# A two-layer graph network on one core: the first layer gathers from a list without its closing loop edges, closed up on the chip, and adds each node's own term from SBUF

## What is computed

```python
# first layer, then x = layernorm(x + feats @ W + b)
m = relu(feat[src]) + 1e-7
a = softmax of m over the edges of each dst, feature by feature
feats = feat + segment_sum(a * m, dst)
# second layer, then x = layernorm(x + h_out)
score = exp(clip(sum over the head of K[src] * Q[dst] / sqrt(12) * (edge_attr @ We + be), -5, 5))
h_out = segment_sum(V[src] * score, dst) / (segment_sum(score, dst) + 1e-6)
```

## Time and profile before

| quantity | value |
|---|---|
| time, median of 3 runs | 4857.5 us (4850.16 to 4858.55) |
| span of the profiled execution | 4892.4 us |
| instructions | 43885 |
| first layer, from the first gather to its last one's start | 2.90 to 2383.50 us |
| second layer's first gather | 2404.94 us |
| busy: POOL, PE, DVE, ACT | 64%, 63%, 47%, 18% of the span |

### The profile page before, as it was taken

One profiled execution on the slowest core, in us unless ns is written; L12 is line 12 of the kernel. 1 busy time (PEld: TensorE's weight loads), 2 busy tenths in 40 slices (PEclk: granted clock), 3 DMA queues, 4 the chain that ended last, 5 costly groups with the idle time before them and its releaser, 6 DMA issues.

```text
span 4892.4 us, 43885 instructions
## 1 busy us (share of the span) xinstructions
PE 3098.1 (63%) x13152; PEld 2767.9 (57%) x13152; DVE 2300.2 (47%) x5605; ACT 870.5 (18%) x1966; POOL 3143.9 (64%) x3330
## 2 busy tenths in 40 slices
PE   3445444555555455455578777878777877877777
PEld 3344434444444444444477677767677777767676
DVE  5434344334433443344445555555555555555555
ACT  1222222222222222222201111111111111111111
POOL 6666666666666666666566666666666666666665
PEclk8666666666656667656665655565666565566665
DMA  3111111121111111111244444444444444444443
GB/s 97 40 40 43 42 39 40 40 45 40 40 44 41 39 40 45 40 39 40 67 111 111 114 112 114 112 111 117 112 111 111 114 112 114 112 114 110 115 113 98
DMA packets 290371, 383.51 MB, mean 78 GB/s; under 512 B 154382, under 2 KB 196911, under 8 KB 290127
## 3 DMA queue, kind: packets, MB, share of 16 engines
q0 software_dynamic: 132864, 251.83, 21.4%
q1 hardware_dynamic: 157263, 128.81, 9.5%
HBM read 360.62 MB, written 19.72 MB: 78 GB/s over the span
## 4 chain that ended last, share of the span: by engine, by line
POOL 31%; issue 23%; PE 18%; another core or an unknown queue 15%; DVE 9%; DMA 2%; ACT 2%; DVEq 0%; SPq 0%; ACTq 0%
POOL rows L454 31%; PE banks L605 4%; PE banks L586 4%; PE banks L577 4%; PE banks L547 3%; DVE onehot L817 2%; PE banks L596 2%; DMA rows<-in_x,src_i 1%; DVE sums L942 1%; DVE ex L930 1%; DMA rows<-key_value,src_i 1%; DVE banks L850 1%; ACT onehot_t L717 1%; DVE sums L940 1%
## 5 line engine op out<-in xcount | busy, mean ns | idle before, releaser
L454 POOL DMA_INDIRECT rows<-key_value,src_i x1661 | 1571.9, 946 | 922.2 <-issue 431.8
L454 POOL DMA_INDIRECT rows<-in_x,src_i x1661 | 1570.6, 946 | 811.6 <-issue 469.1
L547 PE MATMUL banks<-ex,onehot 128*128 128x192 f32 x3322 | 1036.0, 483 | 1026.7 <-DVE ex L930 810.5
L547 PEld LDWEIGHTS banks<-ex,onehot 128*128 128x128 f32 x3322 | 865.2, 288 | 1188.8 <-DVE ex L930 933.9
L586 PE MATMUL banks<-qw,onehot_t 128*128 128x192 f32 x1664 | 609.2, 515 | 401.2 <-ACT onehot_t L717 233.1
L605 PEld LDWEIGHTS banks<-onehot,vals 128*104 128x104 f32 x3322 | 601.2, 272 | 260.2 <-issue 210.3
L605 PE MATMUL banks<-onehot,vals 128*104 128x64 f32 x3322 | 608.2, 359 | 183.8 <-issue 151.5
L586 PEld LDWEIGHTS banks<-qw,onehot_t 128*128 128x128 f32 x1664 | 440.3, 302 | 449.1 <-ACT onehot_t L717 258.4
L577 PE MATMUL banks<-we_sb,ea 97*128 97x96 f32 x3322 | 672.1, 372 | 0.0
L577 PEld LDWEIGHTS banks<-we_sb,ea 97*128 97x128 f32 x3322 | 662.2, 295 | 0.0
L930 DVE SCALAR_TENSOR_TENSOR ex<-banks,ex 128x384 f32<-128x384 f32 x416 | 229.0, 550 | 795.7 <-issue 654.5
(11 more groups left out here) (107 smaller groups left out, 1480.4 us busy)
## 6 DMA issues: line engine op xcount, KB each, us to landing
ea<-in_edge_t SPq DMA_DIRECT2D x415, 192.0 KB
rows<-in_x,src_i POOLq DMA_INDIRECT x1661
rows<-key_value,src_i POOLq DMA_INDIRECT x1661
qw<-query SPq DMA_DIRECT2D x832, 24.0 KB
key_value<-qkv SPq DMA_DIRECT2D x24, 400.0 KB
x<-in_x SPq DMA_DIRECT2D x7, 672.0 KB, 8.2
query<-qkv SPq DMA_DIRECT2D x24, 192.0 KB
out<-outs SPq DMA_DIRECT2D x24, 192.0 KB
```

Of the source, the lines that this page charges most:

```text
L454: pool.indirect_dma_start(out=to[0:n, r, u, :], out_offset=None, in_=table, in_offset=bass.IndirectOffsetOnAxis(ap=src_i[0:n, g * G + u:g ...
L547: last = nc.tensor.matmul(ps_sum0[b], onehot[:, r, u, :], ex[:, b, u, :], start=u == 0, stop=u == n - 1)
```

## The change

1. The edges from group PLAIN = 44 on (edge 22,528) are cut into 128 runs of RUN = 1485 edges, one per partition, the last one filled up with 108 spare loops. Two tables of these runs and the first node of each run are new inputs; SP loads them at the start, behind the weights (three DMAs).
2. During groups 2 to 40 of the first layer DVE works on them between its other instructions. `find_ends` packs source and (dst - first node of the run) in one integer and zeroes the closing edge of each node. `close_up` moves each kept edge down by the number of dropped ones ahead of it, in BITS = 7 steps of powers of two, four instructions each over 1485 elements. PE turns the closed-up runs over (`turn_runs`, 11 transposes), and `list_edges` makes the new source list `src_c`, lanes, group bases and a set of checks from it. A run keeps at most CAP = 1408 edges, so the rest of the first layer has NC0 = 352 groups of four full tiles in place of 372.
3. Each engine's If over the first layer ends at group 44; a second one, on the new flag `unequal`, holds the rest and the second layer. From group 44 POOL gathers by `src_c`, waiting for `s_sum` >= g - PACE + 1 as before.
4. For each chunk ACT computes the own terms (relu and exp of `x1`, `own_terms`), and DVE adds them to the ring just ahead of `messages` (`add_own`). The order of the node work is written for the new groups (`last0`, `at0`, `stage0`); the first four chunks come at groups 46, 54, 62 and 70.
5. DVE's tables of lanes and halves at the start cover 44 groups in place of 416, and the zeroing of `qw` moves to group 45. `qw`, `prod`, `vals` and `outs` become parts of one buffer, `late`, which the work of point 2 uses first.

The second layer's code is as before.

```diff
+PLAIN = 44
+E0 = PLAIN * G * P
+RUN = -(-(EDGES - E0) // P)
+PADR = RUN * P - (EDGES - E0)
+BLK = 11
+CAP = BLK * P
+NC0 = P * BLK // G
+NG0 = PLAIN + NC0
+BITS = 7
+LOW = 14
...
+            sp.dma_start(run_dst[:, :], run_dst_in).then_inc(s_runs, 16)
+            sp.dma_start(packed[:, :], run_src_in).then_inc(s_runs, 16)
+            sp.dma_start(run_first[:, :], run_first_in.to_broadcast([P, P])).then_inc(s_runs, 16)
...
-                for g in range(R0, NG):
+                for g in range(R0, PLAIN):
                     pool.wait_ge(s_sum, min(g - PACE, 2 * (g - R0)) + 1)
                     gather(g, g % R0, xr, x, s_row[g % R0])
+                pool.nop(nofuse=True)
+            with pool.If(1 - unequal(pool, POOL_ENGINE)):
+                pool.wait_ge(s_list, 1)
+                for g in range(PLAIN, NG0):
+                    pool.wait_ge(s_sum, g - PACE + 1)
+                    gather_listed(g)
...
+                    if g == 27:
+                        turn_runs()
...
+                def own_terms(c):
+                    n = tiles_of_chunk(c)
+                    if c:
+                        act.wait_ge(s_owned, c)
+                    nc.scalar.activation(own[:, 0:n, D:W0], x1[:, first_tile(c):first_tile(c) + n, :],
+                                         ACT.Relu).then_inc(s_ownr, 1)
+                    act.wait_ge(s_ownr, c + 1)
+                    nc.scalar.activation(own[:, 0:n, 0:D], own[:, 0:n, D:W0], ACT.Exp,
+                                         bias=gneg[:, :]).then_inc(s_own, 1)
...
-            V.memset(qw[:, :, :], 0.0)
+            V.memset(bound[:, :], 0.0)
...
+                    if g == 2:
+                        dve.wait_ge(s_runs, 48)
+                        link(V.tensor_tensor(step_to, run_dst[:, 1:RUN + 1], run_dst[:, 0:RUN], ALU.subtract))
...
+                def find_movers(k):
+                    link(V.tensor_scalar(bit, packed, 2 ** (LOW + k), None, ALU.bitwise_and))
+
+                def lift_movers():
+                    link(V.scalar_tensor_tensor(out=moved[:, 0:RUN], in0=bit, scalar=0.0, in1=packed,
+                                                op0=ALU.is_gt, op1=ALU.mult))
+
+                def leave_others():
+                    link(V.tensor_tensor(stays, packed, moved[:, 0:RUN], ALU.subtract))
+
+                def set_movers(k):
+                    to = packed if k < BITS - 1 else packed_f
+                    last = V.tensor_tensor(to, stays, moved[:, 2 ** k:2 ** k + RUN], ALU.add)
...
+                for g in range(PLAIN):
+                    weigh_rows(g)
...
+                    if g < 9:
+                        find_ends(g)
+                    elif g < 27:
+                        close_up(g)
                     else:
...
+                        list_edges(g)
...
+                def add_own(c, n_added):
+                    n = tiles_of_chunk(c)
+                    part = own[:, 0:n, 0:D]
+                    dve.wait_ge(s_own, c + 1)
+                    if c < RINGC:
+                        link(V.tensor_tensor(part, part, unlike[:, c * CT:c * CT + n].unsqueeze(2).to_broadcast(
+                            [P, n, D]), ALU.mult))
+                    link(V.scalar_tensor_tensor(out=own[:, 0:n, D:W0], in0=own[:, 0:n, D:W0], scalar=EPS_MSG,
+                                                in1=part, op0=ALU.add, op1=ALU.mult))
+                    dve.wait_ge(s_add, n_added)
+                    V.tensor_tensor(slots(c, n), slots(c, n), own[:, 0:n, :], ALU.add).then_inc(s_owned, 1)
+                    dve.wait_ge(s_owned, c + 1)
...
-                        if last_group(c) == at:
-                            dve.wait_ge(s_add, at + 1)
+                        if at0(c) - 1 == at:
+                            add_own(c, min(at + 1, NG0))
+                        if at0(c) == at:
+                            dve.wait_ge(s_add, min(at + 1, NG0))
                             messages(c)
```

More of the change, by code:

```diff
@@ L150, in build @@
         flag = sb("flag", [1, 1], I32)
+        ends = [0]
+        for size in (RE * 2 * D, 2 * G * D, 2 * G * W1, 2 * CT * D):
+            ends.append(ends[-1] + size)
+        qw = late[:, ends[0]:ends[1]].rearrange("p (a b) -> p a b", b=2 * D)
+        prod = late[:, ends[1]:ends[2]].rearrange("p (a b c) -> p a b c", b=G, c=D)
+        vals = late[:, ends[2]:ends[3]].rearrange("p (a b c) -> p a b c", b=G, c=W1)
+        outs = late[:, ends[3]:ends[4]].rearrange("p (a b c) -> p a b c", b=CT, c=D)
+        spread = qkv[:, :, :, :].rearrange("p a b c -> p (a b c)")
+        beside = rows[:, :, :, :].rearrange("p a b c -> p (a b c)")[:, R0 * G * D:R0 * G * D + RUN]
+        run_dst = late[:, RUN:2 * RUN + 1].bitcast(I32)
+        packed = late[:, 0:RUN].bitcast(I32)
+        packed_f = late[:, 0:RUN]
+        step_to = beside
+        bit = beside.bitcast(I32)
+        moved = spread[:, 0:RUN + 2 ** (BITS - 1)].bitcast(I32)
+        stays = late[:, RUN:2 * RUN].bitcast(I32)
+        listed = beside[:, 0:CAP].bitcast(I32)
+        dst_c = late[:, RUN:RUN + CAP].bitcast(I32)
+        lane_c = spread[:, 0:CAP].bitcast(I32)
+        span_c = spread[:, 0:CAP]
+        empty = late[:, 0:CAP]
+        done0 = spread[0:1, RUN + 64:RUN + 64 + NG0].bitcast(I32)
+        base_f = spread[0:1, RUN + 64 + NG0:RUN + 64 + NG0 + NC0]
+        ahead0 = ahead[0:1, 0:NG0]
         xr = rows[:, :, :, :].rearrange("p a b c -> p (a b c)")[:, 0:R0 * G * D].rearrange(
@@ L457, in gather_tile, with gather_listed @@
                 ).then_inc(s, 16)
+            def gather_listed(g):
+                for u in range(G):
+                    t = (g - PLAIN) * G + u
+                    pool.indirect_dma_start(
+                        out=xr[:, g % R0, u, :], out_offset=None, in_=x,
+                        in_offset=bass.IndirectOffsetOnAxis(ap=src_c[:, t:t + 1], axis=0)
+                    ).then_inc(s_row[g % R0], 16)
             def gather(g, r, to, table, s):
@@ L540, in turn_sums, with sum_rows @@
                 last.then_inc(s_z, 1)
-            with pe.If(1 - irregular(pe, PE_ENGINE)):
[L543 to L549, removed]
+            def sum_rows(g):
+                b, r = g % 2, g % RO
+                pe.wait_ge(s_p, g + 1)
+                for u in range(G):
+                    last = nc.tensor.matmul(ps_sum0[b], onehot[:, r, u, :], ex[:, b, u, :],
+                                            start=u == 0, stop=u == G - 1)
+                last.then_inc(s_sum, 1)
@@ new lines, in slot_values, with add_rows @@
+            def slot_values(g):
+                return nc.values_load_multi_w_load_instructions(
+                    halves[0:1, g:g + 2, :].rearrange("p a b -> p (a b)"),
+                    engines=[DVE_ENGINE], min_val=0, max_val=(SLOTS - 1) * W0,
+                    skip_runtime_bounds_check_because=why)[1]
+            def add_rows(g, low, high):
+                dve.wait_ge(s_sum, g + 1)
+                if g:
+                    dve.wait_ge(s_add, g)
+                else:
+                    dve.wait_ge(s_zero, 1)
+                acc = sums0[0:WIN, bass.ds(low, W0)]
+                V.tensor_tensor(acc, acc, ps_sum0[g % 2][0:WIN, :], ALU.add)
+                acc = sums0[WIN:P, bass.ds(high, W0)]
+                V.tensor_tensor(acc, acc, ps_sum0[g % 2][WIN:P, :], ALU.add).then_inc(s_add, 1)
```

347 lines of the change are left out of this document (268 added, 79 removed).

## The result

The changed kernel takes 4768.3 us (median of 4 runs, 4765.5 to 4773.5) against 4858.0 us for the kernel before: a ratio of 0.982, 95% interval 0.9806 to 0.9834, or 89.7 us less. The forecast was 4774.5 us, with a range from 4743 to 4815 us.

A forecast was written before the change was run, and what follows sets the result against it. The first layer was taken as bound by POOL's gather issue plus pauses for late PE sums. Terms -110.2 - 3.9 + 16 + 4 + 3 + 2 + 3 + 3 = -83 us gave 4774.5 us, range 4743 to 4815 us.

The forecast's parts named there:

- What the change removes: First layer: 77 fewer gathers at 1.432 us each, -110.2 us; less DVE table work at the start, -3.9 us.
- the pauses go by PE's instructions: Both layers: pauses come every 44 to 47 PE matmuls, not by time, so left-out groups take their share along.
- the prediction's alternative price of 1.248 us: First layer: price per gather if only POOL's issue were saved and not the pauses, -96 us for 77 gathers.
- The start: Before the first exponential: moving `qw` zeroing and shrinking tables from 1664 columns to 176 saves 3.9 us, at least 0.
- Closing up: DVE in the first 44 groups: 85 us of added work, of which 16 us shows, between 0 and 40.
- the catch-up: Groups 9 to 13, POOL waiting for sums: 18.5 us added against 8.4 us free on DVE, 10 us late.
- Its rule: DVE instructions of one input and a constant can hold up POOL's gathers: five instructions, +4 us, 0 to 12.
- No slack behind group 13: First layer: the 10 us late at group 13 are never made up, as the pace has no slack against POOL's issue.
- The Ifs: Group 44: four engines load a flag and branch, +2 us, 0 to 8.
- rival C: Second layer gets longer as its pauses shift to 3.8 us each: +333 us, 5107 us; chance 5%.
- the prediction's sign of being wrong: Second layer: a length that moved by more than 10 us would show the forecast wrong.
- rival B: First 44 groups: the preparation sets the pace, 85 us shows in place of 16, 4843 us; chance 15%.

The follow-up runs named there:

- the run meant for it: Three in place of four one-hot products per group from group 44 on, against the changed kernel, gathers kept: 4135.5 us, ratio 0.9862 (chip 15).
- the run without it: Changed kernel without the closing-up work, 20 whole groups of the old list skipped instead, own terms kept: 4753.6 us, ratio 0.9791 (chip 9).
- the two idle kernels: Kernel without closing up plus 37 idle 1.7 us DVE instructions: sums of two SBUF tables 4143.8 us, reductions of one table 4123.1 us (chip 15).
- the run in PSUM: Changed kernel with the closing up working on a table in four PSUM banks: 4121.1 us, ratio 0.983 (chip 0).
- another edit in the same run: Changed kernel with closing up in PSUM and POOL five groups ahead of the sums instead of three: 4771.8 us, ratio 0.9818 (chip 1).

## Why the prediction was right, by its own steps

**What the change removes.** The term that carries the result, 77 gathers at 1.43 us, came out: from group 44 to the last gather it is -108.6 us between the two profiles of one chip, against -110.2 + 3 + 2 = -105 us forecast for that stretch. That a left-out group takes its share of the pauses with it is shown by the equal price of a gather on chip 9 (1.423 us in both kernels). That the pauses go by PE's instructions wasn't shown: the run meant for it fell on a chip without them. On such a chip a gather costs 1.258 us, near the prediction's alternative price of 1.248 us, and there the change brings 56 us. The prediction knew of one kind of chip only, and that the change was measured on the same kind was luck: where there are no pauses, 56 us would have come of the forecast 83.

**The start.** The first relu begins at 34.38 us in place of 37.61, so DVE's shorter tables gave 3.2 of the 3.9 us. On chip 9 they were lost again: POOL's first gather of group 9 starts at 55.01 us against 55.68 us in the second profile of the kernel before, behind a pause of PE that ends at about the same time in both.

**Closing up.** At group 44 the forecast had -3.9 + 16 + 4 + 3 = +19 us, and +11.2 us was measured. At group 13 the kernel was late by 8.6 us already (88.63 against 80.00 us), so the catch-up was indeed the costly part. The sum of the terms was too large: the preparation costs 9 to 12 us by the run without it, for 23. And the hold-ups were misread. The prediction put 16 us on DVE's order and 4 us on five gathers held up by instructions of one input and a constant, and priced the 21 instructions of `close_up` with two inputs as if gathers didn't mind them. Its rule is right as far as it goes (the gather at 105.43), but 42 gathers take over 1.0 us in the first 44 groups and not five, 21 of them under those 21 instructions. The row that showed it was there: the gather of 1.85 us at 16.74 began under L797, an instruction with two SBUF inputs, and not only under the cast behind it. The step that failed is that reading. How much it is worth depends on the bound: on the chips without pauses 20.7 us between the two idle kernels and 15.5 us back in PSUM, on the chips with pauses 2.8 us at group 44, with another edit in the same run. So how the 9 to 12 us divide into hold-ups and DVE's order there isn't shown.

**No slack behind group 13.** The prediction held that what is late there is never made up, as POOL's issue had no slack. Where the pauses are, the sums set the rate and POOL has some room: the first 176 gathers take 190.6 us against 169.8 us in the kernel before, and those 21 us, together with DVE's order, came to 11 us at group 44. On the chips without pauses the statement fits: the run in PSUM is 13.7 us ahead of the changed kernel at group 44 and 15.5 us at the end.

**The Ifs, the own terms, the second layer.** POOL's first listed gather follows with 0.30 us of idle time as any other: 0 us for the 2 us forecast. The own terms cost 0.7 us by the run without them, for 3; without pauses they weren't left out, and the 13 us of held-up gathers behind group 44 may show there. Between the layers +2.7 us, for +3. The second layer +0.4 us, for 0; rival C is out. Only the first pair of profiles set off the prediction's sign of being wrong (22 us in the second layer), by its long execution. The carry-over from the span to the median, with 35 us between them, was right because that execution was long throughout.

**The sums.** -83 us were forecast, and -89.7 and -94.3 us were measured; the preparation, 8 to 14 us too dear, is most of the difference. Three figures of the prediction don't come out of its own terms. With the own terms at 20 us the high end is 4791.5 us, with the held-up gathers at 12 and the preparation at 40 it is 4806.5 us, and with all three 4823.5 us, but not 4815. Half of rival B's 85 us gives 4801 us and not 4808. And five iterations of `close_up` hold eight instructions, 13.6 us at 1.7 us each and not 14.4. Nothing in the result hangs on them.

**Open.** Why sums are late on two chips and not on the other two isn't settled. Nor is it shown that the chip is the reason, for each was used in one set of runs only. What is shown is the place (the wait on PE's sums), the rate (5.7 us per group) and that POOL's lead doesn't change it. In the timeline with five groups ahead the products are recorded as done at 1009.19 (1008.70 + 0.49), and POOL and DVE, which wait for their sums, go on at 1014.09 and 1014.30. Two things narrow it. The traces hold all 3168 products of the first layer on either kind of chip, but only 291 of the 396 updates of the sums' semaphore on chip 9 against all 396 on chip 0 (the changed kernel). As every time here is of an execution whose span and clock were recorded too, a part of the recording in these waits can't be excluded. And fetching of code, which the prediction named as a possible reason, is not in step with them: between 1000 and 1300 us the kernel before has 12 waits of POOL over 1 us and 10 packets of instructions (chip 9), the changed kernel on chip 0 has none and 13.

## What to carry to other kernels

Before work is put into the idle time of DVE, look at what runs beside it: here an indirect gather on GpSimd was held up by DVE instructions that took both inputs from SBUF, and by the one-input form that takes 0.94 us for 1485 columns. The same instructions with an input in PSUM left it alone. Price a term by what bounds the stage, and check the profiled execution's span against the median before subtracting two profiles, since here it was long by 35 us. A gain from fewer gathers is worth what the bound on that chip makes of it, 94 us or 56 us for one program, and so is a remedy for held-up gathers, which brought 15.5 us where POOL is the bound and nothing that shows where it isn't.

## What the runs showed of the hardware that was not expected

The kernel before runs at 4857 us on two chips and 4193 us on two others, and in the first layer of the changed one the difference shows as POOL's waits for PE's sums: a gather costs 1.42 us on the first two and 1.26 us on the others. The changed kernel's second layer takes 2452 and 2077 us. A gather that begins under a DVE instruction of 1485 columns with two SBUF inputs takes 1.1 to 2.4 us and mostly ends about 0.8 us behind it (95.40 + 1.70 and 96.46 + 1.45 above). One that begins under the one-input form of 0.94 us does the same (105.15 + 0.93 and 105.43 + 1.45). One beside a reduction of 1.7 us, or beside the same instructions with an input in PSUM, takes 0.94 us. The bitwise instruction over 1485 columns takes 0.94 us from SBUF and 1.71 us from PSUM.
